# A graph layer with routed experts: padding by zero rows, rows that carry their own number and gate weight, one record of weights per batch, and the last three chunks routed one by one

## What is computed

```python
x = x + _L0_gnn_ref(_layernorm(x), adj, adj, ...)
x = x + _L0_ffn_ref(_layernorm(x)[None], gamma, beta, Wr, br, W1, b1, W2, b2)[0]

def _gru_cell(x, hstate, Wih, Whh, bih, bhh):      # edge cell and node cell
    r = sigmoid(ir + hr); z = sigmoid(iz + hz); n = tanh(inn + r * hn)
    return (1.0 - z) * n + z * hstate

def _L0_ffn_ref(x, gamma, beta, Wr, br, W1, b1, W2, b2):
    xn = (x - mu) * rsqrt(var + EPS) * gamma + beta
    logits = xn @ Wr + br                          # 8 experts
    top_vals, top_idx = top_k(logits, 2)
    w_full = softmax(top_vals) at top_idx
    for e in range(8):
        y_e = gelu(xn @ W1[e] + b1[e]) @ W2[e] + b2[e]     # 128 -> 256 -> 128
        y = y + y_e * w_full[..., e, None]
    return y
```

## Time and profile before

| | |
|---|---|
| median of 3 runs | 1023.62 us (1022.31 to 1024.62) |
| profiled execution | 1028.6 us, its span 1026.9 |
| busy, share of the span | PE 875.1 (85%), DVE 709.7 (69%), ACT 609.8 (59%), POOL 142.4 (14%) |
| mean granted TensorE clock | 0.935 |
| instructions in the profile | 10850 |
| DMA | 144.70 MB, mean 141 GB/s |

### The profile page before, as it was taken

The page is one execution under the profiler, slowest core; times in us unless marked ns, Lnnn a source line. Parts: engine busy times, 40 slices in busy tenths (PEclk is TensorE's granted clock), DMA queues, the critical chain, the costliest instruction groups (busy, mean ns, idle before and its releaser), DMA issues.

```text
span 1026.9 us, 10850 instructions
## 1 busy us (share of the span) xinstructions
PE 875.1 (85%) x2850; PEld 461.3 (45%) x2850; DVE 709.7 (69%) x1323; ACT 609.8 (59%) x883; POOL 142.4 (14%) x181
## 2 busy tenths in 40 slices
PE   5999999999699899999999999999999930476750
PEld 5634343466574344444444444444554520365640
DVE  6433333352799799999999999999478875223225
ACT  0655554521699788998989989989242421234320
POOL 0000000000010000010000010010004247255650
PEclk9999999999799999999999999999999965699975
DMA  9777767120189946545456475220600001344427
GB/s 277 269 266 266 247 233 255 63 85 16 23 218 331 318 146 167 123 115 137 115 144 188 114 167 120 82 102 1 198 1 24 20 29 52 90 123 118 117 73 202
DMA packets 118232, 144.70 MB, mean 141 GB/s; under 512 B 13600, under 2 KB 72642, under 8 KB 117282
## 3 DMA queue, kind: packets, MB, share of 16 engines
q1 hardware_dynamic: 114402, 136.29, 45.3%
q0 software_dynamic: 3776, 7.77, 2.2%
HBM read 120.75 MB, written 23.28 MB: 140 GB/s over the span
## 4 chain that ended last, share of the span: by engine, by line
PE 32%; issue 26%; DVE 22%; SPq 7%; DMA 4%; ACT 4%; DVEq 3%; POOL 1%; another core or an unknown queue 1%; ACTq 0%; POOLq 0%
PE psum L1626 15%; DVE work L1229 9%; PE psum L1743 5%; PE psum L1709 4%; DVE big L1238 3%; DMA big<-adj_cols_dram 2%; SPq L548 2%; DVEq L1229 2%; SPq L542 2%; SPq L543 1%; DVE big L1543 1%; PE psum L1609 1%; PE psum L1807 1%; ACT work L785 1%; SPq L547 1%
## 5 line engine op out<-in xcount | busy, mean ns | idle before, releaser
L1743 PE MATMUL psum<-big,h 128*128 128x512 f32 (+1 forms) x1092 | 445.2, 569 | 17.7 <-DVE big L1238 17.5
L1743 PEld LDWEIGHTS psum<-big,h 128*128 128x128 f32 x1092 | 206.7, 192 | 255.2 <-issue 178.6
L1238 DVE TENSOR_TENSOR big<-work,big 128x1536 f32<-128x1536 f32 (+1 forms) x182 | 299.4, 1645 | 9.1 <-ACT work L785 3.6
L783 ACT ACTIVATE work<-work,shift 128x1024 f32<-128x1024 f32 (+1 forms) x182 | 197.8, 1087 | 46.1 <-DVE work L1229 43.0
L1626 PE MATMUL psum<-big,h 128*128 128x512 f32 x312 | 146.3, 611 | 0.0
L1229 DVE TENSOR_SCALAR work<-rows,h 128x512 f32<-128x512 f32 x312 | 137.5, 484 | 3.7 <-POOLq L601 3.7
L785 ACT ACTIVATE work<-work,shift 128x512 f32<-128x512 f32 (+1 forms) x182 | 123.0, 676 | 0.0
L580 POOL TENSOR_SCALAR_AFFINE_SELECT big<-big 128x128 f32<-128x128 f32 x50 | 22.9, 459 | 642.3 <-DMA big<-adj_cols_dram 640.1
L779 ACT ACTIVATE work<-rows,h 128x512 f32<-128x512 f32 x156 | 110.2, 706 | 0.0
L1626 PEld LDWEIGHTS psum<-big,h 128*128 128x128 f32 x312 | 56.5, 191 | 68.7 <-issue 68.5
L657 ACT ACTIVATE work<-big 128x2048 bf16<-128x2048 f32 (+1 forms) x42 | 75.0, 1785 | 2.7
(11 more groups left out here) (268 smaller groups left out, 772.9 us busy)
## 6 DMA issues: line engine op xcount, KB each, us to landing
big<-adj_cols_dram SPq DMA_DIRECT2D x30, 2048.0 KB, 8.1
sorted_dram<-zeros SPq DMA_DIRECT2D x16, 838.5 KB, 14.5
big<-adj_cols_dram SPq DMA_DIRECT2D x9, 1024.0 KB, 7.1
big<-adj_cols_dram SPq DMA_DIRECT2D x6, 1536.0 KB, 6.6
rows<-stats_dram SPq DMA_DIRECT2D x1, 4608.0 KB, 27.9
rows<-sorted_dram SPq DMA_DIRECT2D x33, 129.0 KB
rows<-w_dram SPq DMA_DIRECT2D x33, 128.0 KB
rows<-stats_dram SPq DMA_DIRECT2D x1, 3840.0 KB, 21.1
```

Of the source, the lines that this page charges most:

```text
L783: nc.scalar.activation(both, both, ACT.Exp, bias=shift[:, 0:1], scale=-1.0)
L1238: nc.vector.tensor_tensor(wadj[:, k % 2, :, 0:w], wexp[:, (n + k) % SLOTS, :, 0:w], ring[:, bass.ds(place, 1), 0:w].broadcast_to([128, HEA ...
L1743: done = nc.tensor.matmul(sums[i], h[:, t, 0:H], wadj[:, t % 2 if v == "plain" else 0, i, 0:w], start=t == 0, stop=t == TILES - 1)
```

## The change

- A row in `sorted_dram` has 130 floats, not 129: features, the row's number as a float, its gate weight. POOL converts the numbers once, `weigh` writes the weights into the rows, and POOL waits for `l_weights` too before it scatters a set. `sorted_dram` gets 256 more rows, the zero fills are 15 DMAs, not 16, each a little larger.
- Rows behind an expert's real ones stay zero; they are no longer masked. Where each row goes is the larger of its number and a constant spare number, one 128x2 operation (`batch_where`); PE waits for the DMA itself, and POOL waits for `b_where` besides `b_y`. The spare rows of `y_dram` come first.
- w1, w2, b1 and b2 of an expert are one record of 515 floats a partition (264 KB), which SP reads for each batch. The preload of w2 and b2 goes, and so do the `value_load`s on PE and DVE. The ring has NX = 8 places, for which SP waits on `b_y`; NY is 4.
- The second layer has w2 fixed and 256 columns moving (two matmuls); ACT adds b2 (`batch_kept`, new), PE transposes back (`batch_back`, two, new), DVE multiplies by the gate weight, two operations of 128x128.
- The tables have 13 DVE instructions, not 34.
- The combine has six adds, not 52 multiply-adds; the pieces are 6, 9 and 11 tiles, before 9, 9 and 8.
- `SETS` has five sets, not four, and DVE's order in the chunk loop is another. The last two sets have banks 4 and 5 for logits and ranks. ACT does `weigh` before `rows_normed`. PE does raw logits of chunk 5 at the end of c = 6 and those of chunk 6 at c = 7.

```diff
-SETS = ((0, 1), (2, 3), (4, 5), (6,))
-ROW = H + 1
+SETS = ((0, 1), (2, 3), (4,), (5,), (6,))
+ROW = H + 2
...
-NX = 6
+NX = 8
...
-NY = 6
+NY = 4
...
-                    sp.wait_ge(b_turned, n - NX + 1)
-                    sp.wait_ge(b_hid, n - NX + 1)
-                sp.dma_start(w1_ring[:, n % NX, :], w1[bass.ds(e, 1), :, :].squeeze(0)).then_inc(b_in[n % NX], 16)
+                    sp.wait_ge(b_y, n - NX + 1)
+                sp.dma_start(w_ring[:, n % NX, :], experts[bass.ds(e, 1), :, :].squeeze(0)).then_inc(b_in[n % NX], 16)
...
+                pool.wait_ge(l_weights, g + 1)
...
+                pool.wait_ge(b_where, n + 1)
                 pool.wait_ge(b_y, n + 1)
...
+                if due(c, 2) is not None:
+                    weigh(due(c, 2))
                 if due(c, 1) is not None:
                     rows_normed(due(c, 1))
-                if due(c, 2) is not None:
-                    weigh(due(c, 2))
...
+            def batch_kept(n):
+                act.wait_ge(b_down, n + 1)
+                if n >= 2:
+                    act.wait_ge(b_back, n - 1)
+                nc.scalar.activation(y_t[:, n % 2, :], bank[4 + n % 2][:, 0:BATCH], ACT.Identity, bias=b2_of[:, n % NX, :])\
+                    .then_inc(b_kept, 1)
...
             for c in range(BEYOND + 1):
-                if due(c, 2) is not None:
-                    route(due(c, 2))
                 if c < NCH:
...
                     mix(c, 1)
+                    if c >= 1:
+                        nodes_kept(c - 1)
                 if c == 0:
                     centre_router()
...
-                if 1 <= c <= NCH:
+                if due(c, 2) is not None:
+                    route(due(c, 2))
+                if c == NCH:
                     nodes_kept(c - 1)
-                if due(c, 2) is not None:
-                    place(due(c, 2))
-                if due(c, 1) is not None:
-                    deviations(due(c, 1))
                 if c < NCH:
                     dve.wait_ge(act_node, c + 1)
...
+                if due(c, 2) is not None:
+                    place(due(c, 2))
+                if due(c, 1) is not None:
+                    deviations(due(c, 1))
...
-                order.done(nc.vector.tensor_tensor(here, here, keep_i[:, n, :].unsqueeze(2).broadcast_to([128, SIDES, ROW]),
-                                                   ALU.bitwise_and))
-                nc.vector.tensor_tensor(where_i[:, n, :], here[:, :, H], dump_i[:, n, :], ALU.bitwise_or)\
-                    .then_inc(b_masked, 1)
+                nc.vector.tensor_tensor(where_i[:, n, :], batch[:, n % NX, :, H], spare_at[:, n, :], ALU.max)\
+                    .then_inc(b_where, 1)
...
-                nc.vector.tensor_tensor(y_sb[:, n % NY, :, :],
-                                        bank[5 + n % 2][:, 0:SIDES * H].rearrange("p (k d) -> p k d", k=SIDES),
-                                        b2_of[:, bass.ds(e, 1), :].broadcast_to([128, SIDES, H]), ALU.add).then_inc(b_y, 1)
+                for k in range(SIDES):
+                    last = nc.vector.tensor_scalar(y_sb[:, n % NY, k, :], bank[6 + n % 2][:, 128 * k:128 * (k + 1)],
+                                                   batch[:, n % NX, k, H + 1:ROW], None, ALU.mult)
+                last.then_inc(b_y, 1)
...
-                if c == SETS[g][0] and g > 0:
+                if g >= LAST_SET - 1:
+                    pe.wait_ge(dve_edge, NCH)
+                elif c == SETS[g][0] and g > 0:
                     pe.wait_ge(l_slots, g)
...
-                        w2_sb[:, bass.ds(e, 1), a, :].squeeze(1), start=a == 0, stop=a == HALVES - 1)
+                    last = nc.tensor.matmul(bank[4 + n % 2][:, 0:BATCH], w2_of[a][:, n % NX, :], act_h[:, n % 3, a, :],
+                                            start=a == 0, stop=a == HALVES - 1)
```

More of the change, by code:

```diff
@@ L892, in _ @@
                     batch_gelu(n + 2)
+                if 0 <= n + 1 < BATCHES:
+                    batch_kept(n + 1)
         @block.vector
@@ L1370, in largest @@
                                                      ALU.is_equal))
-                own, mixed = (bank[2][:, 64 * k:64 * k + nt * E].rearrange("p (t e) -> p t e", e=E) for k in range(2))
+                own, mixed = (ROUTED_IN[g][:, 64 * k:64 * k + nt * E].rearrange("p (t e) -> p t e", e=E) for k in range(2))
                 dve.wait_ge(l_raw, SETS[g][-1] + 1)
@@ L1492, in _ @@
-            nc.vector.tensor_copy(expert_i, b_expert)
-            two = [128, BATCHES, SIDES]
-            def over_sides(value):
-                return value.unsqueeze(2).broadcast_to(two)
-            nc.vector.scalar_tensor_tensor(out=b_spare, in0=over_sides(batch_at), scalar=float(BATCH),
-                                           in1=dump_at.unsqueeze(1).broadcast_to(two), op0=ALU.mult, op1=ALU.add)
-            order.done(nc.vector.tensor_tensor(b_valid, over_sides(b_left), node_at.unsqueeze(1).broadcast_to(two), ALU.is_gt))
@@ L1539, in _ @@
+                last.then_inc(b_y, 1)
+            for n in range(BATCHES):
+                batch_where(n)
+                batch_y(n)
             for q, (t0, t1) in enumerate(PIECES):
                 dve.wait_ge(c_in[q], 32)
-                for k, weight in enumerate((w_first, w_second)):
-                    for t in range(t0, t1):
-                        last = nc.vector.scalar_tensor_tensor(out=x_kept[:, t, :], in0=y_of[k][:, t, :],
-                                                              scalar=weight[:, t:t + 1], in1=x_kept[:, t, :], op0=ALU.mult,
-                                                              op1=ALU.add)
+                for k in range(2):
+                    last = nc.vector.tensor_tensor(x_kept[:, t0:t1, :], x_kept[:, t0:t1, :], y_of[k][:, t0:t1, :], ALU.add)
@@ L1906, in batch_down, with batch_back @@
             def batch_down(n):
-                e = pe.value_load(expert_i[0:1, n:n + 1], min_val=0, max_val=E - 1)
                 pe.wait_ge(b_act, n + 1)
+                if n >= 2:
+                    pe.wait_ge(b_kept, n - 1)
+                for a in range(HALVES):
+                    last = nc.tensor.matmul(bank[4 + n % 2][:, 0:BATCH], w2_of[a][:, n % NX, :], act_h[:, n % 3, a, :],
+                                            start=a == 0, stop=a == HALVES - 1)
+                last.then_inc(b_down, 1)
+            def batch_back(n):
+                pe.wait_ge(b_kept, n + 1)
                 if n >= 2:
```

207 lines of the change are left out of this document (94 added, 113 removed).

## The result

| | before | after |
|---|---|---|
| median of the first comparison | 1023.05 us (1022.31 to 1024.62, 4 runs) | 1038.9 us (1036.99 to 1045.14, 4 runs) |
| ratio | | 1.0164, 95% interval 1.0116 to 1.0211 |
| the same comparison on another chip | 1025.02 us | 1041.88 us, ratio 1.0172 (1.0141 to 1.0202) |
| profiled span | 1026.9 us | 1043.4 us |

The forecast was 1038.9. Slower was right. That the size fits to the microsecond is luck: the chunk loop cost about 6 us less than forecast, the batch stage gained about 4 less, and what lies ahead of chunk 2, where no difference was forecast, came 2.6 us later in the mean of the traces.

What follows compares the result with a forecast made beforehand. It took DVE's order in the chunk loop, then POOL's scatters, then the batch pitch as the bound. 19.3 + 3.5 − 0.5 − 5 − 2 = +15.3 on the median of 1023.6 gave 1038.9 us; own range 1027 to 1047, 8-in-10 range 1022 to 1049.

Steps and rivals of the forecast that it cites:

- (b): Chunk loop: DVE waits after deviations for ACT's rows and edge gates, 4.4, 5.4 and 3.4 us, together 13.2.
- (c): Chunk loop: place(0) comes after the node step, PE's raw logits and attention wait for it; DVE's edge mix waits, +3.3 us.
- (d): Chunk loop: node gates waited for twice more, 1.7 us each, the old 2.41 wait before the last route gone; +0.8.
- The clock: PE in the chunk loop: new gaps bring some half clock, +3.5 us, the middle between nothing and 6.5.
- The third rival: PE stays at half clock from chunk 3 on: +29.1 us in all, 1052.7 us; chance 0.10.
- (a): Chunk loop: one more set adds a deviations block, 3.5 us, and a route and place, 6.4 less 0.4; 9.5 on DVE.
- POOL's part: End of routing: POOL's scatters end 10.6 us after the last place, before 18.1, giving back 7.5 us.
- the third wait of (b): Chunk 6: after deviations of a four-tile set DVE waits 3.4 us for ACT's rows and gates.
- Routing as a whole: Chunk loop to the last sorted scatter: sorted rows out 19.3 us later, plus 3.5 for PE's clock, +22.8.
- Batch stage: The 66 batch scatters: less work per engine shortens the stage by 5 us, bounds −10 and +2.
- Combine: Last stage: six adds in place of 52 instructions, then held by DMA reads; −2 us, bounds −5 and −0.5.
- Head: Start of the batch stage: masking and value_load leave the path, weight record grows; −0.5 us, between −1 and +0.5.

Runs made afterwards that it cites:

- experiment 4: Changed kernel with ACT normalizing a set's rows one chunk later, behind the next chunk's edge gates; median 1007.85 us against 1003.7 for the kernel before, ratio 1.005.
- experiment 5: Changed kernel with PE counting a set's ranks behind the next chunk's edge matmuls, not ahead of them; median 1046.53 us, ratio 1.0218 to the kernel before.

## Why the prediction came out right

**The waits behind deviations (b)** were right to 0.15 us each (12.8 for 13.2), and experiment 4 shows that they cost nearly their full length (12.3).

**The wait around chunk 4 (c)** was right in kind and wrong in place. +3.3 was forecast for the mix alone; what came is 3.59 + 2.67 − 1.12 = 5.1 in the first trace and 2.28 + 2.67 − 1.12 = 3.8, 4.8 and 4.9 in the three others of the changed kernel. The step said that PE's raw logits wait for place(0). They would have, but PE was held before that, at the ranks, a wait that the prediction didn't name though it stands on PE directly ahead of the edge matmuls of chunk 4. Experiment 5 took that away and the named one appeared, with 5.98 us.

**Node gates (d).** The two waits came, 1.60 us each, in chunks 2 and 4, for 1.7. The other part of (d), the wait of 2.41 ahead of the last route, is gone in the old order with five sets as well, so it goes with the changed order on ACT and PE, not with DVE's. (By its own figures (d) is 2 × 1.7 − 2.41 = 1.0, not 0.8.)

**The clock**, +3.5 as the middle of 0 and 6.5, was put beside the waits, and it isn't there. The three waits of (b), (c) with 4.7 in the mean and the two of (d) come to 12.8 + 4.7 + 3.2 = 20.7; between the two orders with five sets 20.2 were measured. For the same difference (b), (c), (d) without the 2.41, and the clock were forecast at 13.2 + 3.3 + 3.2 + 3.5 = 23.2. What half clock cost is inside (c): 3.0 us of the first trace's 3.59, 1.7 of the second's 2.28. It came behind other gaps too (2.01 and 1.88 for a pair of matmuls after 3.87 us idle at 780.86), but there PE stood again right behind these matmuls, for 4.81 us, so it cost nothing. The rule of the Trainium skill (TensorE: Matmul & The Clock Gate, "Part 1: The HAM clock gate") that an idle TensorE falls to 1.2 GHz holds in these traces behind the gaps of 3.87 and 4.81 us in the first trace and of 5.98 in experiment 5. The gap of 3.70 that ends at 837.34 was followed by full clock, and of two gaps on one piece of code, in chunk 1, that of 2.82 us was followed by half clock and that of 2.61 by full. The third rival, half clock from chunk 3 on, didn't come (0.99 in 801 to 826). That 828 to 850 has 0.83 where before had 0.51 is other work in the same window: the near-empty stretch ahead of the last place lies at 866 to 888 after, and has 0.50.

**The extra set (a) with POOL's part** is the step that failed: forecast 9.5 − 7.5 = +2, and +5.4 in the new order, where the third wait of (b) comes with it; measured −1.3 in the old order, −5.8 in the new. The last place came 7.6 us later instead of 9.5 (4.4 instead of 12.9 in the new order), and POOL ended 8.9 us sooner behind it instead of 7.5 (10.1 in the new). The error is in taking POOL's share as a fixed tail behind DVE's last place. POOL was behind from the place of chunks 4 and 5 on; once that set is split POOL starts 8 of its 16 scatters earlier. And the prediction saw its chain of place, raw logits and attention at chunk 4 only, where with four sets chunk 6 has it too (5.59 us).

**Routing as a whole.** Order 20.2, set −1.3, and −2.0 for the old order with four sets against the kernel before (forecast −2.4, the wait of (d)) make the 16.9 measured, where 22.8 was forecast.

**Batch stage**, forecast −5: −4.0 in the first pair, −0.4 in the second, about −1 over all traces. The step that failed is taking less work for each engine as a part of the way to the floor. It rested on no row.

**Combine** −2, measured −2.5 and −2.3, by the bound that was named (DMA), though not by the cause (fewer instructions). **Head** −0.5, measured −0.3 and +0.4.

So +22.8 for the routing was 5.9 too much against the mean of all traces (16.9), and −5 for the batches about 4 too much the other way. The terms as measured come to about 13.5; the spans differ by some 16, because the changed kernel's traces came to chunk 2 2.6 us later in the mean (755.5 for 752.8). Part of that is the half clock in chunk 1, which one of its four traces has and none of the three with the loop of before; whether the rest belongs to the change isn't shown. The first comparison's profile hid all of this, since its changed run came to chunk 2 6.3 us late and its run of before had the longest batch stage of all.

## What to carry to other kernels

When work is moved on one engine, follow what the other engines do in between in their own fixed order: DVE's deviations were as long as ever, but moved directly ahead of a step that needs ACT, they made ACT's 3 to 4 us of row work a wait for everyone. The new order could be kept and most of the loss repaired on the engine that answers (ACT's rows a chunk later gave back 12.3 us of 20.2); the old order stayed the best. Price a queue's backlog (POOL's 1.27 us a scatter) from when its work becomes available, not from the last piece; and split a difference of one trace pair by stages over several runs before crediting a stage with a gain or a loss, since here 4 us of the batch stage's and 6 of the chunk loop's were the run.

## What the runs showed that I had not expected

A whole stage that runs at one pace on one chip and at another on the next: 83.6 us for 66 scatters in four kernels with the changed stage on one chip, 102.2 to 106.5 in ten traces of both forms on the others, and with it 1003.7 us or 1023 to 1030 for the kernel before. It hides a stage's real bound (POOL at 1.27 us a scatter) on the slower kind. A clock that after nearly the same idle (2.61 and 2.82 us) is full in one run and half in the next, worth 3 us. And a small one: a 128x128 add on DVE at 0.21 us against 0.27 for a multiply-add with a per-partition scalar was worth more than going from 52 instructions to 6.
